# Moving one product of a pair's output projection behind the next scores, and the lower tiles' copies behind two exponentials, in a causal attention kernel in split fp32

## The chip, the cores and the metric

The kernel runs on one core of one Trainium2 chip. The metric is the device time of one execution in microseconds, and the number for the kernel before is the median of three executions, 1481.09 us (1480.62 to 1482.14).

## The reference, cut to what matters

The whole is one transformer block on x of 4 batches x 512 positions x 512 channels: an adaptive layer norm, causal attention with 32 heads of 128 channels (8 key and value heads, each shared by 4 heads) and rotary positions, a gated residual, a second norm, and a mixture over 64 expert biases with the 8 largest router weights. The change lies in the attention:

```python
q = (h @ Wq.T) ...                    # 32 heads of 128, then rotary
scores = einsum('bhqd,bhkd->bhqk', q, k) * scale       # causal
attn = softmax(scores)
out = einsum('bhqk,bhkd->bhqd', attn, v)
return out.reshape(..., 32 * 128) @ Wo.T               # "the projection"
```

All of it is wanted in fp32. The kernel gets this out of fp32r products by splitting each operand into a high and a low part and running three products (low times high, high times low, high times high) for one, which `passes` (line 94) lists.

## The kernel before, in words

**Steps.** Work is cut into 32 units (a key and value head and a batch), each with 4 heads. One head of one unit is a step, t = 0 to 127; h = t % 4, u = t // 4. The loop `for t in range(BY_PE)` is unrolled on each engine, and every engine has its own hand-written order in a function `step(t)`. In one step TensorE computes the scores of head t + 1, the queries of head t + 3 (`q_proj`, 12 products), in steps with h = 1 and 3 the keys and values of the next unit, and parts of what belongs to earlier heads. From step 92 (`FFN_FROM`) on the second half of the block (norm, router, experts), for tiles that are finished, is mixed in as well. The change leaves these later steps as they are.

**Pairs.** After the softmax two heads are handled together as a pair p (heads 2p and 2p + 1). The 512 queries are four tiles of 128: UPPER is tiles 2 and 3, LOWER is tiles 0 and 1. `values_pair(p, UPPER)` writes probabilities times values to the PSUM bank pv in step 2p + 2, `values_pair(p, LOWER)` does the same in step 2p + 3. ScalarE copies the bank to OT_hi (`pair_split_hi`, L1059) and VectorE writes the remainder OT_lo (`pair_split_lo`, L1433). UPPER and LOWER use the same two OT buffers, one after the other. `out_pair(p, UPPER)` (L718) then runs 12 products of 512 columns at the end of step 2p + 3, and `out_pair(p, LOWER)` another 12 in step 2p + 4, into the banks o0 to o3. ScalarE may overwrite OT with LOWER only once the UPPER products have read it: it waits on the semaphore `pe_upper` or `pe_op`, which the last product of tile 3 increments.

**TensorE, one even step t = 2p + 4 (before).** scores(t + 1) in tile order 3, 2, 1, 0 (L649, L645 and, last, L646); q_proj(t + 3) (L589); out_pair(p, LOWER); values_pair(p + 1, UPPER). The scores of tile 3 and the queries share the bank s3, so `q_proj` waits until VectorE has read tile 3's scores (`dve_s`, L1393). `out_pair(p, LOWER)` waits for OT_lo (`dve_o`). An odd step has scores, values_pair LOWER, q_proj, keys or values, out_pair UPPER.

**ScalarE, one even step.** `pair_split_hi` LOWER (L1059); `split_moved_hi(t - 1)` (L1049, two copies of 640 columns from PT_raw to PT_hi); `exponentials(t + 1, 0)` of tiles 3 and 2 (L1028), which wait for VectorE's minima; `exponentials(t + 1, 1)` of tiles 1 and 0; `normalise` (L1035) in two halves, each after VectorE's `invert_sums` (L1400).

**VectorE, one even step.** `mask_and_max(t + 1, 0)` reads the scores of tiles 3 and 2 (L1393); `pair_split_lo` LOWER (L1433); `mask_and_max(t + 1, 1)` of tiles 1 and 0; in h = 2 two sums into y (`add_out`, L1450); `invert_sums`; `q_rope(t + 3)` (L1355 to L1357), which waits for the queries; the transposes of the normalised probabilities in 32 x 32 blocks (L1417).

**The transposed probabilities.** They leave by DMA to DRAM (`store_blocks`, L2010) and come back reordered (`load_transposed`, L2036) as PT_raw. In an odd step t SP issues the eight loads of heads t - 1 and t, four each, as soon as `values_pair` LOWER has finished with the buffers (`pe_pv`). ScalarE splits head t - 1 at the end of the odd step and head t in the next even step (L1049); GpSimd makes the low parts (L1759).

The queues of the engines are in order: an instruction waits for its semaphore and what stands behind it waits too.

Of the kernel before, what the change touches and what calls it, by code (L numbers as in the profile page):

```python
# [12 lines left out]
P = 128  # L13
BATCH, SEQ, HID = 4, 512, 512
HEADS, KV, HD = 32, 8, 128
GROUP = HEADS // KV
# [119 lines left out]
def build(nc, A, out):  # L136
    ctx = ExitStack()
    with ctx:
# [373 lines left out]
        def tensor_program(pe):  # L512
# [159 lines left out]
            def values_pair(p, tiles):  # L672
# [24 lines left out]
                                       start=(kb == 0 and n == 0), stop=(kb == last_key and n == 2))  # L697
                mm.then_inc(pe_pv, 1)

            def out_pair(p, tiles, some=None):  # L700
                u = 2 * p // GROUP
                heads = [2 * p % GROUP, 2 * p % GROUP + 1]
                pe.wait_ge(dve_o, pair_done(p, tiles))
                for h in heads:
                    wait_weights(u, f"wo{h}")
                if p == 0:

                    if tiles == UPPER:
                        pe.wait_ge(dve_r, 6)
                    else:  # L710
                        pe.wait_ge(dve_vt, 2)
                for j in some or tiles:
                    if heads[0] == 0 and 0 < u < LAST_UNIT:
                        pe.wait_ge(dve_y, added(u - 1, j))
                    for h in heads:
                        o_at = (2 * (j - tiles[0]) + h % 2) * P
                        for n, (o, w) in enumerate(passes(OT_of(p, tiles), wo)):
                            mm = pe.matmul(bank[f"o{j}"][:], o[:, o_at:o_at + P], w[:, h, :],  # L718
                                           start=(u < LAST_UNIT and h == 0 and n == 0),
                                           stop=(u < LAST_UNIT - 1 and h == GROUP - 1 and n == 2))  # L720
                    if heads[1] == GROUP - 1:
                        mm.then_inc(pe_op, 1)
                    elif j == UPPER[-1]:
                        mm.then_inc(pe_upper, 1)

            def values_last(t, tiles):
# [77 lines left out]
            def step(t):  # L804
                u, h, n, before = t // GROUP, t % GROUP, ffn_tile(t), ffn_tile(t - 1)
                scores(t + 1, QUERY_ORDER, before, n)
                if h % 2 == 1 and t > 1:
                    values_pair(t // 2 - 1, LOWER)
                if 2 < t < ALL - 3:
                    q_proj(t + 3)  # L810
                if h == 1 and 0 < u < LAST_UNIT:
                    k_proj(u + 1)
                if h == 3 and 0 < u < LAST_UNIT:
                    v_proj(u + 1)

                if t == 0:
                    q_proj(4)
                    k_proj(1)
                if t == 1:
                    v_proj(1)  # L820
                    q_proj(5)
                if h % 2 == 1 and t > 1:
                    out_pair(t // 2 - 1, UPPER)
                if n is not None:
                    pe.wait_ge(dve_s, score_read(t + 1, 0))
                    ffn_mix(early(n - 4), "s1")
                    ffn_logits(early(n - 2), "s2")
                if h % 2 == 0 and t > 2:
                    out_pair(t // 2 - 2, LOWER)
                if n is not None:  # L830
                    tile_waits((mixed, n - 4), last=EARLY_TILES - 1)
                    ffn_transpose(early(n - 1), "s1")
                if h % 2 == 0 and t > 0:
                    values_pair(t // 2 - 1, UPPER if t < ALL - 2 else LOWER)
                if before is not None:
                    pe.wait_ge(dve_s, score_read(t + 1, 0))
                    ffn_weights_T(early(before - 3), "s1")
# [103 lines left out]
        def scalar_program(act):  # L941
# [181 lines left out]
            def step(t):  # L1123
                u, h, n, before = t // GROUP, t % GROUP, ffn_tile(t), ffn_tile(t - 1)
                if h % 2 == 1 and t > 1:
                    pair_split_hi(t // 2 - 1, UPPER)
                if h % 2 == 0 and 2 < t < ALL - 2:
                    pair_split_hi(t // 2 - 2, LOWER)
                if t == 1:
                    split_moved_hi(0)  # L1130
                if h % 2 == 1 and t + 2 < ALL:
                    q_split(t + 2)
                if t == 2:
                    k_split(1)
                if h % 2 == 0 and 0 < t < ALL - 2:
                    split_moved_hi(t - 1)
                if t == ALL - 2:
                    split_moved_hi(t - 2)
                    split_moved_hi(t - 1)
                if n is not None:  # L1140
                    ffn_exp(early(n - 3))
                if t == 0:
                    v_split_hi(0)
                exponentials(t + 1, 0)
                if h == 1 and t > 1:
                    v_split_hi(u)
                exponentials(t + 1, 1)
                if n is not None:
                    ffn_normal(early(n - 1))
                if t == ALL - 3:  # L1150
                    pair_split_hi(PAIRS - 2, LOWER)
                normalise(t + 1, 0)
                if t == 2:
                    q_split(4)
                if h == 2 and 0 < u < LAST_UNIT:
                    k_split(u + 1)
                normalise(t + 1, 1)
                if h % 2 == 1 and 1 < t < ALL - 3:
                    split_moved_hi(t - 1)
                if h % 2 == 1 and 1 < t < ALL - 3:  # L1160
                    q_split(t + 3)
                for g, i in pieces(t):
                    split_chunk(g, i)
                if n is not None:
                    ffn_modulate(early(n - 1), "s1")
                if t - FFN_FROM in EXPERT_STEPS:
                    split_experts(EXPERT_STEPS.index(t - FFN_FROM))
                if t == ALL - 4:
                    make_diagonal()
                if before is not None:  # L1170
                    ffn_weights_copy(early(before - 3), "s1")
# [97 lines left out]
        def vector_program(dve):  # L1269
# [291 lines left out]
            def step(t):  # L1561
                u, h, n, before = t // GROUP, t % GROUP, ffn_tile(t), ffn_tile(t - 1)
                if h % 2 == 1 and t > 1:
                    pair_split_lo(t // 2 - 1, UPPER)
                mask_and_max(t + 1, 0)
                if t == 1:
                    mask_and_max(2, 1)
                    k_rope(1)
                    invert_sums(2, 0)
                    invert_sums(2, 1)  # L1570
                    split_moved_lo(0)
                    transpose_blocks(2)
                    return
                if h % 2 == 0 and 2 < t < ALL - 2:
                    pair_split_lo(t // 2 - 2, LOWER)
                mask_and_max(t + 1, 1)
                if t == ALL - 2:
                    split_moved_lo(t - 1)
                if before is not None:
                    ffn_x1(early(before))  # L1580
                    ffn_stats(early(before))
                if h == 2 and 0 < u < LAST_UNIT:
                    add_out(u - 1, UPPER)
                if h == 3 and 0 < u < LAST_UNIT:
                    add_out(u - 1, LOWER)
                if t == 2:
                    q_rope(4)
                invert_sums(t + 1, 0)
                if h == 1:
                    v_split_lo(u)  # L1590
                if 2 < t < ALL - 3:
                    q_rope(t + 3)
                invert_sums(t + 1, 1)
                if t == 0:
                    v_split_lo(0)
                if t == ALL - 3:
                    pair_split_lo(PAIRS - 2, LOWER)
                if h % 2 == 1:
                    transpose_blocks(t + 1, QUERY_ORDER[:2])
                if h == 1 and u + 1 < UNITS:  # L1600
                    k_rope(u + 1)
                if h == 3 and u + 1 < UNITS:
                    transpose_values(u + 1)
                if n is not None:
                    finish(early(n - 4), "s1")
                    ffn_top(early(n - 3))
                    ffn_bias(early(n - 2), "s2")
                    keep(early(n - 3))
                if h % 2 == 1:
                    transpose_blocks(t + 1, QUERY_ORDER[2:])  # L1610
                elif moved(t + 1):
                    transpose_blocks(t + 1)
                if t in (0, 2):
                    q_rope(t + 3)
# [631 lines left out]
```

## Time and profile before

| | before |
|---|---|
| median of 3 runs | 1481.09 us |
| the profiled execution, its own time | 1481.78 us |
| span of its trace, first to last instruction | 1480.1 us |
| TensorE busy (matmuls) | 1451.2 us, 98% |
| VectorE busy | 1160.1 us, 78% |
| GpSimd busy | 1023.6 us, 69% |
| ScalarE busy | 1005.0 us, 68% |
| granted TensorE clock, mean | 0.996 |

1.7 us of the profiled execution's own time lie outside the span. Busy time is the union of the records of an engine; matmuls overlap in the records (each is drawn some 390 ns long while the next starts 230 ns later), so a busy TensorE can still lose time between the starts of two products. That is why the rows below are start times of single products.

### The profile page before, as it was taken

Reading aid. Unit: us, or ns where it says so; the run is one execution under the profiler, and the core shown is the slowest. Engines: PE = TensorE matmul, PEld = TensorE weight load, DVE = VectorE, ACT = ScalarE, POOL = GpSimd, SP = SyncE. Lnnn points to the kernel's source line nnn. Section 1 sums busy time; section 2 is a strip of 40 time slices with the busy share of each in tenths; the row PEclk is TensorE's granted clock in tenths of the full one; section 3 lists DMA queues with packets and bytes.
Section 4 is the critical chain, followed back from the end, with each engine's and each line's share of the span. In section 5 each row is a group of like instructions: output and inputs, shape, how many; then the busy total and the mean of one; then the engine's idle time right before and its main releaser. Section 6 shows DMA issues by size and latency. Waiting matters only on the chain.

```text
span 1480.1 us, 24295 instructions
## 1 busy us (share of the span) xinstructions
PE 1451.2 (98%) x7012; PEld 1211.3 (82%) x7012; DVE 1160.1 (78%) x3549; ACT 1005.0 (68%) x2381; POOL 1023.6 (69%) x802
## 2 busy tenths in 40 slices
PE   7997999999999999999999999999999999999997
PEld 4686888888888888888888888888888888888876
DVE  5867777777777777777777777777779988988866
ACT  2467776776767776777677766767677676776674
POOL 1656776776667776677678666767588888886662
PEclk9999999999999999999999999999999999999999
DMA  9647775776766676578667756669788899889881
GB/s 328 205 126 255 223 229 144 213 224 182 202 216 214 181 223 188 172 219 237 182 184 222 220 168 199 213 180 254 224 248 252 270 293 260 278 263 266 268 228 51
DMA packets 214820, 322.02 MB, mean 218 GB/s; under 512 B 42248, under 2 KB 132104, under 8 KB 214688
## 3 DMA queue, kind: packets, MB, share of 16 engines
q1 hardware_dynamic: 214352, 320.34, 72.3%
q8 instruction: 57, 0.93, 0.3%
q14 instruction: 75, 0.61, 0.1%
q10 hardware_dynamic: 336, 0.12, 0.0%
HBM read 179.43 MB, written 140.95 MB: 216 GB/s over the span
## 4 chain that ended last, share of the span: by engine, by line
PE 90%; DVE 5%; issue 2%; ACT 2%; POOL 1%; DMA 0%; SPq 0%; DVEq 0%; ACTq 0%; POOLq 0%
PE bank_s L589 22%; PE bank_o L718 22%; PE bank_pv L696 14%; PE bank_s L649 13%; PE bank_s L617 6%; PE bank_s L602 5%; PE bank_s L560 2%; PE bank_o L523 1%; PE bank_s L645 1%; PE bank_s L771 1%; DVE blocks L1417 1%; ACT probs L1028 1%; PE bank_pv L589 1%; DMA wup_in<-in_wup 0%; PE bank_s L646 0%
## 5 line engine op out<-in xcount | busy, mean ns | idle before, releaser
L1759 POOL TENSOR_TENSOR PT_lo<-PT_raw,PT_hi 128x640 fp32r<-128x640 f32 x246 | 382.1, 1574 | 27.0 <-ACT PT_hi L1049 27.0
L1035 ACT ACTIVATE probs<-probs,row_inv 128x512 f32<-128x512 f32 (+3 forms) x512 | 258.0, 553 | 195.2 <-DVE row_inv L1400 195.1
L1747 POOL TENSOR_TENSOR rot_c<-rot_c,rot_s 128x512 f32<-128x512 f32 x128 | 166.0, 1297 | 274.3 <-DVE rot_s L1357 274.3
L1028 ACT ACTIVATE probs<-probs,row_min 128x512 f32<-128x512 f32 (+3 forms) x512 | 281.8, 552 | 52.2 <-DVE row_min L1393 52.1
L1417 DVE STREAM_TRANSPOSE blocks<-probs 128x384 f32<-128x384 f32 x508 | 213.9, 447 | 18.7 <-ACT probs L1035 12.4
L649 PE MATMUL bank_s<-kT_both,qT_hi 128*128 128x512 f32 (+2 forms) x768 | 214.9, 341 | 1.2 <-POOL qT_lo L1752 0.6
L1393 DVE CUSTOM_DVE_ANT_0 probs<-bank_s,mask 128x512 f32<-128x512 f32 (+2 forms) x384 | 203.5, 552 | 0.4
L589 PE MATMUL bank_s<-hT_lo,wq_hi 128*128 128x512 f32 x488 | 196.5, 403 | 2.5 <-DVE row_min L1393 1.2
L1752 POOL TENSOR_TENSOR qT_lo<-rot_c,qT_hi 128x512 fp32r<-128x512 f32 x128 | 166.6, 1301 | 42.2 <-ACT qT_hi L1010 41.3
L718 PE MATMUL bank_o<-wo_lo,OT_hi 128*128 128x512 f32 x496 | 194.4, 392 | 0.0
L718 PE MATMUL bank_o<-wo_hi,OT_hi 128*128 128x512 f32 x496 | 193.3, 390 | 0.0
L718 PE MATMUL bank_o<-wo_hi,OT_lo 128*128 128x512 f32 x496 | 192.9, 389 | 0.0
L589 PE MATMUL bank_s<-hT_hi,wq_hi 128*128 128x512 f32 x488 | 191.3, 392 | 0.0
L589 PE MATMUL bank_s<-hT_hi,wq_lo 128*128 128x512 f32 x488 | 190.4, 390 | 0.0
L1049 ACT ACTIVATE PT_hi<-PT_raw 128x640 fp32r<-128x640 f32 x250 | 169.7, 728 | 12.9 <-DMA PT_raw<-blocks 12.4
L649 PEld LDWEIGHTS bank_s<-kT_both,qT_hi 128*128 128x128 f32 x768 | 142.6, 188 | 17.3 <-DVE kv_rot L1366 1.8
L1433 DVE TENSOR_TENSOR OT_lo<-bank_pv,OT_hi 128x512 fp32r<-128x512 f32 x124 | 85.4, 688 | 83.7 <-ACT OT_hi L1059 83.7
L696 PE MATMUL bank_pv<-PT_lo,v_hi 128*128 128x512 f32 x374 | 138.8, 371 | 9.6 <-issue 5.5
L1355 DVE TENSOR_TENSOR rot_c<-bank_s,cos_t 128x512 f32<-128x512 f32 x122 | 84.2, 690 | 80.8 <-PE bank_s L589 78.3
L696 PE MATMUL bank_pv<-PT_hi,v_hi 128*128 128x512 f32 x374 | 133.9, 358 | 0.0
L696 PE MATMUL bank_pv<-PT_hi,v_lo 128*128 128x512 f32 x374 | 133.8, 358 | 0.0
L649 PE MATMUL bank_s<-kT_both,qT_lo 128*128 128x512 f32 (+2 forms) x384 | 129.3, 337 | 0.0
(296 smaller groups left out, 3216.6 us busy)
## 6 DMA issues: line engine op xcount, KB each, us to landing
blocks<-blocks SPq DMA_DIRECT2D x127, 640.0 KB, 3.4
PT_raw<-blocks SPq DMA_DIRECT2D x500, 160.0 KB, 3.9
stage<-in_wq SPq DMA_DIRECT2D x32, 256.0 KB, 5.1
vblocks<-kv_raw SPq DMA_DIRECT2D x32, 256.0 KB, 5.4
kv_raw<-vblocks SPq DMA_DIRECT2D x128, 64.0 KB, 2.1
stage<-in_wo SPq DMA_DIRECT2D x32, 256.0 KB, 5.0
split_wq<-wq_hi SPq DMA_DIRECT2D x32, 256.0 KB, 5.4
split_wq<-wq_lo SPq DMA_DIRECT2D x32, 256.0 KB, 5.7
```

Source lines behind the costliest of these rows:

```text
L589: mm = pe.matmul(q_bank(t)[:], w[:, h, c, :], x[:, b * CH + c, :], start=(c == 0 and n == 0), stop=(c == CH - 1 and n == 2))
L649: mm = pe.matmul(score_bank[qt], q, k[:, 0:keys], start=(n == 0), stop=(n == 2))
L696: mm = pe.matmul(to[:, :, (first - tiles[0]) * SUB:], a[:, kb, :], ps, start=(kb == 0 and n == 0), stop=(kb == last_key and n == 2))
L718: mm = pe.matmul(bank[f"o{j}"][:], o[:, o_at:o_at + P], w[:, h, :], start=(u < LAST_UNIT and h == 0 and n == 0), stop=(u < LAST_UNIT - 1 a ...
L1028: ins = act.activation(row(t, qt), row(t, qt), ACT.Exp, bias=row_min[m][:, qt:qt + 1], scale=-1.0, accum_out=row_sum[m][:, qt:qt + 1])
L1035: ins = act.activation(row(t, qt), row(t, qt), ACT.Copy, scale=row_inv[t % 2][:, qt:qt + 1])
L1049: act.activation(parts_of(t)[0][:, at], raw_of(t)[:, at], ACT.Copy).then_inc(act_t, 1)
L1393: dve.tensor_tensor_reduce(row(t, qt), score_bank[qt], row(t, 0) if qt == 0 else mask[:, SEQ - (qt + 1) * P:], -SCALE, -LOWEST, ALU.add, A ...
L1417: ins = dve.transpose(blocks_v[:, qt:qt + 3 * whole_keys - 2:3], keys[:, 0:whole_keys])
L1747: pool.tensor_tensor(rot_c[:], rot_c[:], rot_s[:], ALU.add).then_inc(pool_a, 1)
L1752: pool.tensor_tensor(lo[:], rot_c[:], hi[:].bitcast(F32), ALU.subtract).then_inc(pool_q, 1)
L1759: pool.tensor_tensor(lo[:, at], raw_of(t)[:, at], hi[:, at].bitcast(F32), ALU.subtract).then_inc(pool_t, 1)
```

## The change

In the even steps 4 to 90, the product high times high of the second head on tile 3 of `out_pair(p, UPPER)` is no longer issued at the end of step 2p + 3 but in step 2p + 4, between the scores and the queries. The increment of `pe_upper` or `pe_op` goes with it. ScalarE's copy of the LOWER pair moves from the front of the even step to behind `exponentials(t + 1, 0)`; VectorE's remainder moves from between the two halves of `mask_and_max` to behind both. From step 92 on all stays as it was. No instruction is added or removed.

```diff
+            def upper_in_two(p):
+                return 2 * p + 4 < FFN_FROM
+
             def out_pair(p, tiles, some=None):
...
                     for h in heads:
-                        o_at = (2 * (j - tiles[0]) + h % 2) * P
-                        for n, (o, w) in enumerate(passes(OT_of(p, tiles), wo)):
-                            mm = pe.matmul(...)
-                    if heads[1] == GROUP - 1:
+                        put_off = j == UPPER[-1] and h == heads[1] and upper_in_two(p)
+                        out_head(p, tiles, j, h, range(2) if put_off else range(3))
+
+            def out_head(p, tiles, j, h, which):
+                u = 2 * p // GROUP
+                o_at = (2 * (j - tiles[0]) + h % 2) * P
+                for n, (o, w) in enumerate(passes(OT_of(p, tiles), wo)):
+                    if n in which:
+                        mm = pe.matmul(...)
+                if 2 in which:
+                    if h == GROUP - 1:
                         mm.then_inc(pe_op, 1)
-                    elif j == UPPER[-1]:
+                    elif h == 1 and j == UPPER[-1]:
                         mm.then_inc(pe_upper, 1)
...
# TensorE, step(t)
                 if h % 2 == 1 and t > 1:
                     values_pair(t // 2 - 1, LOWER)
+                if h % 2 == 0 and t > 2 and upper_in_two(t // 2 - 2):
+                    p = t // 2 - 2
+                    out_head(p, UPPER, UPPER[-1], 2 * p % GROUP + 1, range(2, 3))
                 if 2 < t < ALL - 3:
                     q_proj(t + 3)
# ScalarE, step(t)
-                if h % 2 == 0 and 2 < t < ALL - 2:
+                if h % 2 == 0 and FFN_FROM <= t < ALL - 2:
                     pair_split_hi(t // 2 - 2, LOWER)
...
                 exponentials(t + 1, 0)
                 if h == 1 and t > 1:
                     v_split_hi(u)
+                if h % 2 == 0 and 2 < t < FFN_FROM:
+                    pair_split_hi(t // 2 - 2, LOWER)
                 exponentials(t + 1, 1)
# VectorE, step(t)
-                if h % 2 == 0 and 2 < t < ALL - 2:
+                if h % 2 == 0 and FFN_FROM <= t < ALL - 2:
                     pair_split_lo(t // 2 - 2, LOWER)
                 mask_and_max(t + 1, 1)
+                if h % 2 == 0 and 2 < t < FFN_FROM:
+                    pair_split_lo(t // 2 - 2, LOWER)
```

## Rows read from the trace of the kernel before

**Rows 1.** The page's busy time of each engine: busy us (share of the span) xinstructions.

```profile
PE 1451.2 (98%) x7012; PEld 1211.3 (82%) x7012; DVE 1160.1 (78%) x3549; ACT 1005.0 (68%) x2381; POOL 1023.6 (69%) x802
```

**Rows 2.** Timeline of TensorE around step 50: start us, length, engine, line, operation, tiles.

```profile
613.43 0.39 PE L718 MATMUL bank_o<-wo_hi,OT_hi 128*128 128x512 f32 x1
613.65 0.39 PE L649 MATMUL bank_s<-kT_both,qT_hi 128*128 128x512 f32 x1
...
615.34 0.22 PE L646 MATMUL bank_s<-kT_both,qT_lo 128*128 128x128 f32 x1
615.52 0.47 PE L589 MATMUL bank_s<-hT_lo,wq_hi 128*128 128x512 f32 x1
615.83 0.40 PE L589 MATMUL bank_s<-hT_hi,wq_lo 128*128 128x512 f32 x1
...
618.34 0.39 PE L718 MATMUL bank_o<-wo_lo,OT_hi 128*128 128x512 f32 x1
```

**Rows 3.** The same view, odd step 51: scores, then a product that waits for nothing.

```profile
625.17 0.22 PE L646 MATMUL bank_s<-kT_both,qT_lo 128*128 128x128 f32 x1
625.23 0.45 PE L696 MATMUL bank_pv<-PT_lo,v_hi 128*128 128x512 f32 x1
625.52 0.39 PE L696 MATMUL bank_pv<-PT_hi,v_lo 128*128 128x512 f32 x1
```

**Rows 4.** The same view, even step 48, the shorter kind of wait.

```profile
594.49 0.22 PE L646 MATMUL bank_s<-kT_both,qT_lo 128*128 128x128 f32 x1
594.62 0.47 PE L589 MATMUL bank_s<-hT_lo,wq_hi 128*128 128x512 f32 x1
```

**Rows 5.** Timeline of ScalarE and VectorE, step 50 to the start of step 51.

```profile
613.91 0.60 ACT L1059 ACTIVATE OT_hi<-bank_pv 128x512 fp32r<-128x512 f32 x1 [0.59 <-PE bank_o L718]
614.41 1.35 ACT L1049 ACTIVATE PT_hi<-PT_raw 128x640 fp32r<-128x640 f32 x2
...
615.29 0.08 DVE L1393 DVE_READ_ACCUMULATOR2_ANT row_min<- 128x1 f32 x1
...
615.78 0.69 DVE L1433 TENSOR_TENSOR OT_lo<-bank_pv,OT_hi 128x512 fp32r<-128x512 f32 x1
...
617.14 1.28 DVE L1450 TENSOR_TENSOR y<-bank_o,y 128x512 f32<-128x512 f32 x2
...
623.69 0.60 ACT L1059 ACTIVATE OT_hi<-bank_pv 128x512 fp32r<-128x512 f32 x1 [0.34 <-PE bank_pv L696]
...
624.32 0.69 DVE L1433 TENSOR_TENSOR OT_lo<-bank_pv,OT_hi 128x512 fp32r<-128x512 f32 x1 [1.34 <-ACT OT_hi L1059]
```

**Rows 6.** Timeline of ScalarE in step 20, where the load of PT_raw is late.

```profile
301.58 1.37 ACT L1049 ACTIVATE PT_hi<-PT_raw 128x640 fp32r<-128x640 f32 x2 [0.65 <-DMA PT_raw<-blocks]
302.86 0.71 ACT L1028 ACTIVATE probs<-probs,row_min 128x512 f32<-128x512 f32 x1
...
303.56 0.60 ACT L1028 ACTIVATE probs<-probs,row_min 128x384 f32<-128x384 f32 x1
```

**Rows 7.** The same view: first and last of the ten even steps with such a wait.

```profile
176.02 1.37 ACT L1049 ACTIVATE PT_hi<-PT_raw 128x640 fp32r<-128x640 f32 x2 [0.33 <-DMA PT_raw<-blocks]
...
845.15 1.37 ACT L1049 ACTIVATE PT_hi<-PT_raw 128x640 fp32r<-128x640 f32 x2 [0.76 <-DMA PT_raw<-blocks]
```

**Rows 8.** ScalarE's waits from 155 to 1050 us: us in total, times, longest.

```profile
ACT PT_hi L1049 <- DMA PT_raw<-blocks: 6.6, 16, 0.8
```

**Rows 9.** The view of tile PT_raw around step 50, issues and landing.

```profile
L2036 SPq DMA_DIRECT2D PT_raw<-blocks x8: 303/432/1172, 605.7 to 609.6; - x8
...
DMA to landing us min/median/max: 2.5/3.6/4.4
```

**Rows 10.** DMA queues from 295 to 297 us (step 20): packets, MB, share.

```profile
q8 instruction: 1, 0.02, 4.2%
```

**Rows 11.** Timeline of TensorE in step 4.

```profile
133.02 0.22 PE L646 MATMUL bank_s<-kT_both,qT_lo 128*128 128x128 f32 x1
134.43 0.47 PE L589 MATMUL bank_s<-hT_lo,wq_hi 128*128 128x512 f32 x1 [1.18 <-DVE row_min L1393]
```

More of the change, by code:

```diff
@@ L715, in out_pair @@
                     for h in heads:
-                        o_at = (2 * (j - tiles[0]) + h % 2) * P
-                        for n, (o, w) in enumerate(passes(OT_of(p, tiles), wo)):
-                            mm = pe.matmul(bank[f"o{j}"][:], o[:, o_at:o_at + P], w[:, h, :],
-                                           start=(u < LAST_UNIT and h == 0 and n == 0),
-                                           stop=(u < LAST_UNIT - 1 and h == GROUP - 1 and n == 2))
-                    if heads[1] == GROUP - 1:
+                        put_off = j == UPPER[-1] and h == heads[1] and upper_in_two(p)
[5 more added lines that the diff above has]
+                    if n in which:
+                        mm = pe.matmul(bank[f"o{j}"][:], o[:, o_at:o_at + P], w[:, h, :],
+                                       start=(u < LAST_UNIT and h == 0 and n == 0),
+                                       stop=(u < LAST_UNIT - 1 and h == GROUP - 1 and n == 2))
+                if 2 in which:
+                    if h == GROUP - 1:
                         mm.then_inc(pe_op, 1)
-                    elif j == UPPER[-1]:
+                    elif h == 1 and j == UPPER[-1]:
                         mm.then_inc(pe_upper, 1)
```

## The prediction

> **What bounds the kernel now.** I read the page's busy times first: TensorE is busy for 98% of the span, no other engine for more than 78% [rows 1]. So a gain can only come from the spacing of TensorE's products, and a loss from any wait put in front of them. About 0.2%, 3 us, is what a measurement of this kernel can tell from no change.
>
> Then I went through TensorE's timeline step by step. Every time below is against T, the start of the last score product (L646) of an even step; in step 50, T = 615.34. There the first query product starts at T + 0.18 and the second 0.31 later [rows 2]. In an odd step the product behind the scores waits for nothing: it starts 0.06 after L646 and the next 0.29 later [rows 3] (0.284 as the mean over the odd steps; from here on three digits are means over the start times of all steps of a kind, of which one row stands). The even step's wait is for VectorE: its reading of tile 3 ends at 615.29 + 0.08 = T + 0.03 [rows 5], and TensorE starts 0.15 us after that. Of the 44 even steps that the change touches (4 to 90), 29 look like step 50, 13 have the shorter wait of step 48, 0.13 to 0.14 us [rows 4], and two (4 and 46) are irregular.
>
> **What is gained.** With the moved product in front, the order is L646, 0.06, moved product, 0.284, first query, 0.23, second query. The 0.23 that it took at the end of the odd step (613.43 to 613.65 [rows 2]) is gone there. Before, from L646 to the third query: 0.181 + 0.314 + 0.230, and 0.227 in the odd step, 0.952. After: 0.060 + 0.284 + 0.230 + 0.230 = 0.804. Gain 0.148. In the 13 shorter steps 0.096. The wait itself is hidden: it lets go at about T + 0.15 and the query now wants to start at T + 0.34. Sum: 29 x 0.148 + 13 x 0.096 = 5.5 us. Steps 4 and 46 give nothing: there VectorE itself is late, and the first query starts when VectorE lets it, in step 4 at T + 1.41 [rows 11]. Bounds: 5.5 us, and 0 if VectorE's read of tile 3 slips by as much as TensorE comes earlier; the nearest row is step 50, where that read begins behind a wait for TensorE, so I take 5.5.
>
> **The copies that move.** This is the other half, and I cost it by the chain that `out_pair` LOWER waits for. Today ScalarE copies LOWER at T - 1.43 (613.91), VectorE's remainder is done at 615.78 + 0.69 = T + 1.13 [rows 5], and the LOWER products start at 618.34 = T + 3.00 [rows 2]. There are 1.9 us of slack. After the change the copy stands behind three things on ScalarE: two PT copies, 1.27 us from the start of the first to the exponential (301.58 to 302.86), then the exponentials of tile 3, 0.71 to the start of the next (302.86 to 303.56), and tile 2, 0.60 [rows 6]. Then: OT_hi 0.60, hand-over 0.03 (623.69 + 0.60 to 624.32), OT_lo 0.69 [rows 5], and 0.15 to TensorE (the hand-over above). From the start of an exponential of tile 3 to the first LOWER product: 0.71 + 0.60 + 0.60 + 0.03 + 0.69 + 0.15 = 2.78 us. TensorE gets there at T + 0.06 + 0.28 + 12 x 0.229 = T + 3.09. So the exponential must start by T + 0.31.
>
> *When the loads are on time it does.* It then waits only for the minima, until about T + 0.07. The PT copies do not hold it: around step 50 the last load is issued at 609.6 and lands at most 4.4 us later [rows 9], at 614.0, T - 1.3. That load is released by the odd step's `values_pair`, and one product fewer now lies between that and T, so in the new frame it lands at T - 1.1, the PT copies end at T + 0.17, and 0.14 to 0.24 us are left.
>
> *When the loads are late it does not.* In ten of the 44 steps ScalarE, having finished OT_hi at T - 0.83, sits idle for d before it can start the PT copies: 0.33, 0.44, 0.20, 0.65, 0.66, 0.43, 0.50, 0.17, 0.21 and 0.76 us (steps 8, 16, 18, 20, 40, 42, 52, 60, 64, 72), 4.35 in all; step 20's row and the first and last of them are shown [rows 6, 7]. They are ten of the 16 waits of this kind [rows 8]; the other six are in odd steps or ahead of the even heads' copies and are not lengthened. Today these waits cost TensorE nothing, because the LOWER copy is ahead of them. Now it is behind: the exponential starts at T - 0.83 + d + 0.23 (the shorter frame) + 1.27 = T + 0.67 + d, and TensorE waits 0.36 + d. Sum: 10 x 0.36 + 4.35 = 7.9 us. In step 72 OT_hi ended 0.1 later than elsewhere, which makes 8.0.
>
> Loads that land inside the time that OT_hi covers today show no idle time. They cost from 0 up to 0.36 in each of 32 steps, 0 to 11 us. The nearest row is the load of step 50, which leaves a margin, so most cost nothing; for a handful of later ones (some 0.1 to 0.2 each) I take 0.7. A pipeline that restarts after a wait loses some 0.03 (0.314 against 0.284): 10 x 0.03 = 0.3. Step 4 is late in the loads as well as in VectorE: between 0 and 1.9 (today's slack); ScalarE's PT copies there end late enough that I take 1.4. Loss: 8.0 + 0.7 + 0.3 + 1.4 = 10.4 us.
>
> **What else moves.** VectorE's later work in an even step starts when OT_lo ends, T + 2.7 instead of T + 1.9. In h = 2 this delays the 1.28 us of `add_out`, the rotation and ScalarE's normalising by some 0.8; VectorE idles 1.34 us ahead of the next step's remainder [rows 5], so the transposes and the store still end in time, and I cost it at nothing; without that cover it would be 0.8 x 22 = 18 us. `add_out` now needs the moved product, which ends near T + 0.5, before VectorE can be there. `values_pair` UPPER needs the bank pv free at T + 5.7, 3 us after OT_lo. On GpSimd and SP nothing is moved.
>
> **Sum.** 10.4 - 5.5 = 4.9 us slower. Against the profiled execution, 1481.78 us, that is 1486.7; it ran 0.7 above the median, so 1486.0.
>
> **Rivals.**
>
> *A: the loads land early enough and the gain stays.* What lets a load be late? In step 20 one packet of 16 KB of the instruction queue runs in the middle of the loads [rows 10]. For A: late loads could be chance, fewer in the next program, or the margin 0.3 larger than I made it from single rows. If all ten were on time, 5.5 - 0.7 - 1.4 (step 4) = 3.4 to 5.5 us are gained: 1475.6 to 1477.7. Against A: ScalarE's wait would have to vanish from ten steps, and even d = 0 costs 0.36. Chance 0.17. The Trainium skill ("Runtime: NRT & Kernel Launch", Instruction fetch mechanics) says that crossing a 16 KiB block of instructions is one tail bump of the queue, "mostly hidden". By that rule the fetch would delay nothing and case A's time would hold; the trace shows the fetch among loads that are late, so I give it no more than A's chance.
>
> *B: gain and loss cancel.* If the chain is 0.2 to 0.3 shorter per step than my sum (a PT copy that starts sooner), the ten waits cost 5 to 6 us and steps at the margin nothing: from 3 faster to 3 slower, 1478.1 to 1484.1. Chance 0.22. The point from which it decides is a start of the exponential at T + 0.55 instead of T + 0.31.
>
> *C: every step waits.* The margin in steps with loads on time is only 0.15 to 0.25 us. If ScalarE or the hand-overs take 0.3 more than I read, 32 further steps wait 0.1 to 0.3 us: some 6 us more, 1490 to 1494. Chance 0.06.
>
> *D: the change does nothing*, because the query's wait is not the one for tile 3. The irregular step 4 names VectorE's minimum as what is waited for [rows 11], so this is inside B.
>
> The forecast has 0.55: 3 to 8.4 us slower, 1484.1 to 1489.5. Slower 0.55 + 0.06 = 0.61, same 0.22, faster 0.17. The range goes from 1477.5 to 1489.5: below it lies most of A (0.14), above it C (0.06).
>
> **What would show it.** Right: the product L718 between L646 and L589, the first query 0.34 after L646 without a wait; a new wait of L718 for DVE OT_lo (L1433), ten to fifteen times, up to 1.2 us, in the same steps in which ScalarE waits for PT_raw; some 9 us in all. Wrong: no such waits (A), waits in nearly all even steps (C), or the first query still late behind VectorE.

## The result and the profile after

The changed kernel takes 1484.45 us (median of 20 runs, 1480.36 to 1486.29) against 1481.05 us for the kernel before (20 runs, 1479.42 to 1482.75): a ratio of 1.0020, 95% interval 1.0013 to 1.0027. By the medians it is 3.4 us slower, at the near end of the 3 to 8.4 us of the forecast. The single run that was profiled took 1483.30 us (span 1481.6), below that median, so the trace shows less of the loss than the median has. The changed kernel also scatters more: 5.9 us from fastest to slowest instead of 3.3.

The page after. TensorE's busy time has fallen while the span has grown: the time without a product record went from 28.9 us (1480.1 - 1451.2) to 32.6 (1481.6 - 1449.0). The chain that ended last has changed as well; DMA has 5% of it, where it had 0% before:

```profile
PE 1449.0 (98%) x7012; PEld 1207.1 (81%) x7012; DVE 1155.9 (78%) x3549; ACT 1004.8 (68%) x2381; POOL 1023.5 (69%) x802
...
PE 82%; DVE 5%; DMA 5%; ACT 4%; SPq 2%; issue 2%; POOL 0%; DVEq 0%; ACTq 0%; POOLq 0%
PE bank_o L729 21%; PE bank_s L589 18%; PE bank_pv L696 14%; PE bank_s L649 12%; PE bank_s L617 4%; PE bank_s L602 4%; DMA PT_raw<-blocks 4%; SPq L2055 2%; PE bank_s L560 2%; ACT probs L1043 2%; PE bank_o L523 1%; PE bank_s L645 1%; PE bank_s L783 1%; ACT PT_hi L1064 1%; DVE OT_lo L1450 1%
```

The loads of PT_raw hold 4% of that chain now, with ScalarE's and VectorE's work behind them (L729 is the old L718, L1064 the old L1049, L1074 the old L1059, L1450 the old L1433). The next rows are TensorE's waits from 120 to 1060 us: us in total, times, longest.

```profile
PE bank_o L729 <- DVE OT_lo L1450: 3.4, 7, 0.8
```

The kernel before has no such wait. The view draws a wait only where it is longer than the overlap of the records, so I also took the start times of all products: in 12 of the 44 steps the first LOWER product comes later than 0.23 after the last query product, by 5.7 us in all, the longest 1.0. ScalarE's waits from 155 to 1050 us show what stands in front; against [rows 8] the wait for the loads has gone from 6.6 to 33.0 us. Most of it is time in which ScalarE used to copy LOWER, and costs nothing:

```profile
ACT PT_hi L1064 <- DMA PT_raw<-blocks: 33.0, 46, 1.3
```

**A step with its load on time**, step 50 again: timelines of TensorE, ScalarE and VectorE. These answer to [rows 2, 5].

```profile
616.67 0.22 PE L646 MATMUL bank_s<-kT_both,qT_lo 128*128 128x128 f32 x1
616.73 0.45 PE L729 MATMUL bank_o<-wo_hi,OT_hi 128*128 128x512 f32 x1
617.02 0.39 PE L589 MATMUL bank_s<-hT_lo,wq_hi 128*128 128x512 f32 x1
...
619.77 0.39 PE L729 MATMUL bank_o<-wo_lo,OT_hi 128*128 128x512 f32 x1
```

```profile
615.67 1.37 ACT L1064 ACTIVATE PT_hi<-PT_raw 128x640 fp32r<-128x640 f32 x2 [0.79 <-DMA PT_raw<-blocks]
616.95 0.71 ACT L1043 ACTIVATE probs<-probs,row_min 128x512 f32<-128x512 f32 x1
...
618.25 0.58 ACT L1074 ACTIVATE OT_hi<-bank_pv 128x512 fp32r<-128x512 f32 x1
...
618.86 0.69 DVE L1450 TENSOR_TENSOR OT_lo<-bank_pv,OT_hi 128x512 fp32r<-128x512 f32 x1 [0.85 <-ACT OT_hi L1074]
```

With T = 616.67: moved product at T + 0.06, first query at T + 0.35 without a wait, LOWER at T + 3.10. The PT copies start at T - 1.00, the exponential at T + 0.28, and OT_lo is done at T + 2.88. That is 0.22 before TensorE's arrival; less the hand-over of 0.06 (below) 0.16 are left, within the 0.14 to 0.24 that the prediction gave. In the other steps of this trace whose LOWER products don't wait, 0 to 0.34 are left.

**A step with a late load**, step 64: TensorE, then ScalarE and VectorE, then the chain that ended last in the same stretch.

```profile
762.92 0.22 PE L646 MATMUL bank_s<-kT_both,qT_lo 128*128 128x128 f32 x1
762.98 0.45 PE L729 MATMUL bank_o<-wo_hi,OT_hi 128*128 128x512 f32 x1
763.27 0.39 PE L589 MATMUL bank_s<-hT_lo,wq_hi 128*128 128x512 f32 x1
...
765.79 0.39 PE L589 MATMUL bank_s<-hT_hi,wq_hi 128*128 128x512 f32 x1
766.80 0.50 PE L729 MATMUL bank_o<-wo_lo,OT_hi 128*128 128x512 f32 x1 [0.62 <-DVE OT_lo L1450]
767.14 0.40 PE L729 MATMUL bank_o<-wo_hi,OT_lo 128*128 128x512 f32 x1
```

```profile
762.87 1.37 ACT L1064 ACTIVATE PT_hi<-PT_raw 128x640 fp32r<-128x640 f32 x2 [1.16 <-DMA PT_raw<-blocks]
764.14 0.70 ACT L1043 ACTIVATE probs<-probs,row_min 128x512 f32<-128x512 f32 x1
...
765.45 0.57 ACT L1074 ACTIVATE OT_hi<-bank_pv 128x512 fp32r<-128x512 f32 x1
...
766.05 0.69 DVE L1450 TENSOR_TENSOR OT_lo<-bank_pv,OT_hi 128x512 fp32r<-128x512 f32 x1 [1.85 <-ACT OT_hi L1074]
```

```profile
756.70 6.14 DMA PT_raw<-blocks
...
762.87 0.64 ACT PT_hi L1064
...
764.24 1.30 ACT probs L1043 x4
765.54 0.49 ACT OT_hi L1074
...
766.05 0.70 DVE OT_lo L1450
...
766.80 3.01 PE bank_o L729 x12
```

The load takes 6.14 us to land (4.4 at most in [rows 9]), ScalarE starts the PT copies at T - 0.05 instead of T - 1.00, and the LOWER products start 1.01 after the last query product instead of 0.23: a wait of 0.78. One packet of the instruction queue runs here too: by its record it starts at 756.56, 0.14 before the load is issued, and takes 1.29 us (DMA queues, 755 to 757.5 us):

```profile
q8 instruction: 1, 0.02, 3.2%
```

### The profile page after: what moved, and what is told of

It is laid out like the page before. It is cut to its first block, busy times and chain, and to the rows that moved or that the text cites. A ratio compares the mean times of both kernels' runs of the same rounds, so it can differ in the third digit from the quotient of the medians.

```text
span 1481.6 us, 24295 instructions
## 1 busy us (share of the span) xinstructions
PE 1449.0 (98%) x7012; PEld 1207.1 (81%) x7012; DVE 1155.9 (78%) x3549; ACT 1004.8 (68%) x2381; POOL 1023.5 (69%) x802
## 4 chain that ended last, share of the span: by engine, by line
PE 82%; DVE 5%; DMA 5%; ACT 4%; SPq 2%; issue 2%; POOL 0%; DVEq 0%; ACTq 0%; POOLq 0%
PE bank_o L729 21%; PE bank_s L589 18%; PE bank_pv L696 14%; PE bank_s L649 12%; PE bank_s L617 4%; PE bank_s L602 4%; DMA PT_raw<-blocks 4%; SPq L2055 2%; PE bank_s L560 2%; ACT probs L1043 2%; PE bank_o L523 1%; PE bank_s L645 1%; PE bank_s L783 1%; ACT PT_hi L1064 1%; DVE OT_lo L1450 1%
## 5 line engine op out<-in xcount | busy, mean ns | idle before, releaser
L729 PE MATMUL bank_o<-wo_lo,OT_hi 128*128 128x512 f32 x496 | 196.3, 396 | 5.7 <-DVE OT_lo L1450 3.4
L1064 ACT ACTIVATE PT_hi<-PT_raw 128x640 fp32r<-128x640 f32 x250 | 170.1, 729 | 39.2 <-DMA PT_raw<-blocks 38.5
L729 PE MATMUL bank_o<-wo_hi,OT_hi 128*128 128x512 f32 x496 | 196.3, 396 | 0.0
L589 PE MATMUL bank_s<-hT_lo,wq_hi 128*128 128x512 f32 x488 | 193.4, 396 | 1.9 <-DVE row_min L1410 0.9
L729 PE MATMUL bank_o<-wo_hi,OT_lo 128*128 128x512 f32 x496 | 193.1, 389 | 0.0
L1450 DVE TENSOR_TENSOR OT_lo<-bank_pv,OT_hi 128x512 fp32r<-128x512 f32 x124 | 85.6, 690 | 128.7 <-ACT OT_hi L1074 128.7
```

The source lines that it names most:

```text
L589: mm = pe.matmul(q_bank(t)[:], w[:, h, c, :], x[:, b * CH + c, :], start=(c == 0 and n == 0), stop=(c == CH - 1 and n == 2))
L1064: act.activation(parts_of(t)[0][:, at], raw_of(t)[:, at], ACT.Copy).then_inc(act_t, 1)
```

## The experiments

The change once more, the copies alone, the product alone and the other product put off were timed together, with the kernel before at 1481.51 us; the remaining four together on another chip, with it at 1482.29 us. Differences are between medians of the same session.

**The change once more.**

> The changed kernel once more, to see whether the waits of the LOWER products come back in the same steps. Theory (the LOWER copy stands behind a late load of PT_raw): 10 to 14 waits of out_pair for OT_lo, most of them again in steps 8, 20, 40, 42, 60, 64 and 84, their sum 5 to 8 us, and a time 2 to 5 us above the kernel before. Rival (the waits are chance of one execution): fewer than half of those steps wait again.

1486.02 us against 1481.51, ratio 1.0027 (1.0019 to 1.0036). Its trace has waits in 16 steps, 6.6 us in all; 11 of the first trace's 12 steps (4, 6, 8, 16, 20, 28, 40, 42, 60, 64, 84, and not 66) are among them. So the waits are tied to places in the program, but each one's size changes by some tenths: 1.0 us in step 8 of the first trace and 0.2 in the second. That would widen the scatter, but it is not shown to be all of it: the kernel with the product alone, where no LOWER product waits, scatters by 4.7 us over 11 runs. By the medians the change is 4.5 us slower here, near the forecast's 4.9.

**Only the copies moved.**

```diff
             def upper_in_two(p):
-                return 2 * p + 4 < FFN_FROM
+                return False
```

> Only the LOWER copies move, the product stays at the end of the odd step. Theory: the loss stays and the gain is gone; the queries wait again for tile 3 (first query 0.18 after the last score product), the LOWER products still wait after late loads, a little less each since the load is 0.23 earlier against the scores: 4 to 7 us above the kernel before, 1485 to 1488. Rival 1 (the product's new place costs the time, the copies are harmless): within 1 us of the kernel before. Rival 2 (the copies cost only because the product shortens the frame): 1 to 2 us above.

1487.54 us, ratio 1.0033 (1.0021 to 1.0046): 6.0 us slower than before. TensorE's waits from 120 to 1060 us:

```profile
PE bank_o L729 <- DVE OT_lo L1450: 4.3, 10, 0.7
```

By start times 11 steps wait, 6.2 us in all (the profiled run, 1489.38, is the slowest of the six). The kernel is slower without the product too, and its ratio can't be told from the 1.0027 with it. Both rivals fall: the copies are not harmless by themselves, and the product is not what costs. The gain is missing here, so the copies' own loss is 6.0 us, against 9.8 (4.5 + 5.3, below) beside the moved product; the late steps' shorter frame would make such a difference, but the intervals are too wide to show it.

**Only the product moved.**

```diff
# ScalarE and VectorE, step(t): both copies back where they were
-                if h % 2 == 0 and FFN_FROM <= t < ALL - 2:
+                if h % 2 == 0 and 2 < t < ALL - 2:
                     pair_split_hi(t // 2 - 2, LOWER)
...
-                if h % 2 == 0 and 2 < t < FFN_FROM:
-                    pair_split_hi(t // 2 - 2, LOWER)
```

> Only the product moves; ScalarE's LOWER copy is again ahead of the PT copies and so waits for the moved product until about 0.45 after the last score product, and holds back the PT copies and all exponentials of the step by some 1.9 us. Theory: no product of out_pair waits for OT_lo; the gain of 3 to 5 us shows unless the late exponentials reach TensorE through the stores and loads: 1477 to 1479. Rival (the product's place itself costs): 1481 or more, with the first query late. Second rival (late exponentials matter): above 1483, with waits of values_pair for PT_lo or of scores.

1481.70 us, ratio 0.9996 (0.9987 to 1.0005): no change, and outside the expected 1477 to 1479. The time is that of the first rival, but its sign is not there: the first query starts 0.35 after L646 in all steps but 4 and 46. No LOWER product waits. The second rival's time (above 1483) did not come, but a wait of the scores, which it named, did. The trace shows a new short stop in the steps with h = 2, here between steps 50 and 51, on GpSimd and on TensorE:

```profile
622.22 1.29 POOL L1783 TENSOR_TENSOR kT_both<-kv_raw,kT_both 128x512 fp32r<-128x512 f32 x1 [0.74 <-ACT kT_both L1031]
```

```profile
623.30 0.28 PE L696 MATMUL bank_pv<-PT_hi,v_hi 128*128 128x256 f32 x1
623.61 0.47 PE L649 MATMUL bank_s<-kT_both,qT_hi 128*128 128x512 f32 x1
623.92 0.39 PE L649 MATMUL bank_s<-kT_both,qT_lo 128*128 128x512 f32 x1
```

The same on GpSimd and the first score product in the kernel before:

```profile
621.69 1.31 POOL L1768 TENSOR_TENSOR kT_both<-kv_raw,kT_both 128x512 fp32r<-128x512 f32 x1 [0.74 <-ACT kT_both L1016]
```

```profile
623.49 0.39 PE L649 MATMUL bank_s<-kT_both,qT_hi 128*128 128x512 f32 x1
```

The scores of the next unit need the low part of its keys. Before, it is done at 621.69 + 1.31 = 623.00, 0.49 ahead of them; now at 622.22 + 1.29 = 623.51, and they start 0.31 after the product before them instead of 0.12, the next one 0.31 later instead of 0.23. ScalarE's LOWER copy waits for the moved product and starts at 615.81 instead of 613.91, the PT copies behind it are late, GpSimd's PT_lo starts at 617.11 instead of 616.59, and the keys queue up behind that.

**The product moved in the steps with h = 0 alone.**

```diff
             def upper_in_two(p):
-                return 2 * p + 4 < FFN_FROM
+                return 2 * p + 4 < FFN_FROM and p % 2 == 0
```

(on top of the kernel with the product alone moved)

> As the kernel with the product alone moved, but only in the even steps with h = 0 (22 of 44); in those with h = 2 it stays in the odd step. Theory (what product_only gives back is the wait of the next unit's first scores for the low part of the keys on GpSimd, which the late PT copies push back in steps with h = 2): the half without keys keeps its gain, 22 x 0.12 = 2.6 us, 1478 to 1479.5. Rival (the give-back is spread over all steps): within 1 us of the kernel before.

1478.97 us, ratio 0.9980 (0.9971 to 0.9989), 3.3 us faster than before. Half the steps give more than all 44 do. What comes back is lost from h = 2 on, as the trace said: by the starts of the scores, the product alone in all 44 steps is 0.25 us slower per unit in steps h = 2 and 3 than the kernel with the other product put off (below), and no slower in h = 0 and 1.

**ScalarE's chain 0.60 shorter.**

```diff
-                exponentials(t + 1, 0)
...
                 if h % 2 == 0 and 2 < t < FFN_FROM:
+                    exponentials(t + 1, 0, (3,))
                     pair_split_hi(t // 2 - 2, LOWER)
+                    exponentials(t + 1, 0, (2,))
```

> As the changed kernel, but ScalarE's LOWER copy goes behind the exponential of tile 3 alone, so 0.60 us earlier. Theory (the waits are the part of load lateness plus chain that exceeds TensorE's arrival): every wait is 0.60 shorter; of the 12 to 16 waits three to five are left, 1 to 2 us in all, and the gain shows: 1477 to 1479. Rival (the waits have another cause than the length of ScalarE's chain, such as VectorE's order): the time stays at 1484 to 1487.

1479.19 us, ratio 0.9978 (0.9969 to 0.9987), 0.2 us above what was expected. TensorE's waits, 120 to 1060 us:

```profile
PE bank_o L729 <- DVE OT_lo L1454: 1.0, 3, 0.7
```

By start times six steps wait, 2.0 us in all, three of them under 0.3. The loads are as late as before (ScalarE waits 34.0 us for them in this trace). So the length of the chain decides what a late load costs.

**ScalarE's chain 0.50 longer.**

```diff
                 if h % 2 == 0 and 2 < t < FFN_FROM:
+                    exponentials(t + 1, 1, (1,))
                     pair_split_hi(t // 2 - 2, LOWER)
-                exponentials(t + 1, 1)
+                    exponentials(t + 1, 1, (0,))
```

> As the changed kernel, but the LOWER copy goes behind the exponential of tile 1 too, 0.50 us later. Theory: the waits that there are grow by 0.5 each (14 x 0.5 = 7 us) and the margin of the steps with loads on time is used up, so that some 30 more steps wait 0.1 to 0.3 us and pay a restart of 0.15 each: 10 to 18 us above the changed kernel, 1495 to 1503. Rival (only late loads matter, the margin is wider): 7 us above, 1492.

1503.01 us, ratio 1.0144 (1.0130 to 1.0158), 20.7 us slower than before, at the end of what was expected.

```profile
PE bank_o L729 <- DVE OT_lo L1454: 13.8, 23, 1.3
```

By start times all 44 steps wait, 21.7 us in all, the shortest 0.15. So the margin in steps with loads on time was at most 0.35 us, and rival C of the prediction, waits in every step, lay one short operation away.

**The other product put off.** In this version the high times high product stays in the odd step and the one that reads OT_lo (low times high) is put off instead. ScalarE's OT_hi is free when the odd step ends, and both LOWER copies go back to their old places. Only VectorE, writing OT_lo, waits for the moved product (`upper_done(p)` in the cut below counts what the pairs before p have added to `pe_upper`).

```diff
             def out_head(p, tiles, j, h, which, low_last=False):
...
+                products = passes(OT_of(p, tiles), wo)
+                if low_last:
+                    products = [products[0], products[2], products[1]]
...
+                        if low_last and n == 1:
+                            mm.then_inc(pe_upper, 1)
...
# ScalarE, pair_split_hi
+                if tiles == LOWER and 2 * p + 4 < FFN_FROM:
+                    act.wait_ge(pe_upper, upper_done(p) + 1)
...
# VectorE, pair_split_lo
+                if tiles == LOWER and 2 * p + 4 < FFN_FROM:
+                    if p % 2 == 0:
+                        dve.wait_ge(pe_upper, upper_done(p) + 2)
+                    else:
+                        dve.wait_ge(pe_op, QT * (p // 2) + 2)
```

> The product put off is the one with the low part of OT (low times high), the high times high one stays in the odd step, and both LOWER copies are back at their old places. ScalarE overwrites OT_hi once the high products have read it, only VectorE's OT_lo waits for the moved product, until about 0.5 after the last score product, when it would start anyway (0.44). Theory: the gain of 3 to 5 us without the loss, 1476 to 1478, no wait of out_pair for OT_lo. Rival (the product's place itself costs): 1481 or more.

1475.79 us, ratio 0.9959 (0.9946 to 0.9971): 5.7 us faster than before and 10.2 faster than the change on the same chip. TensorE and VectorE in step 50 (L740 is the projection, L1468 OT_lo):

```profile
612.22 0.22 PE L654 MATMUL bank_s<-kT_both,qT_lo 128*128 128x128 f32 x1
612.27 0.46 PE L740 MATMUL bank_o<-wo_hi,OT_lo 128*128 128x512 f32 x1
612.57 0.40 PE L597 MATMUL bank_s<-hT_lo,wq_hi 128*128 128x512 f32 x1
```

```profile
612.71 0.08 DVE L1423 DVE_READ_ACCUMULATOR2_ANT row_min<- 128x1 f32 x1
612.84 0.69 DVE L1468 TENSOR_TENSOR OT_lo<-bank_pv,OT_hi 128x512 fp32r<-128x512 f32 x1
```

The moved product fills TensorE's gap. OT_lo starts 0.13 after the minimum is read out; before, both start at 615.78. So the new wait costs VectorE about 0.1 us. No LOWER product waits. From step 3 to step 90 TensorE comes out 5.4 us ahead of the trace before, of which 0.3 is an irregular stop in step 46 that this run did not have, while one in step 84 cost it 0.2.

**The same, in the later steps too.** The three bounds of 92 became 124.

> low_last with the product put off in the 16 even steps from 92 to 122 as well, where the first query starts 0.11 to 0.49 after the last score product. If the wait for tile 3 is hidden there too: 16 x 0.12 to 0.25 = 2 to 4 us less than low_last, 1472 to 1474. Rival (VectorE, busier in these steps, is late for other reasons and sets the pace): the same as low_last, 1475 to 1477.

1476.06 us, ratio 0.9958 (0.9946 to 0.9971), not to be told from the version above. In the trace the product is in its new place in the late steps (first query 0.35 after the last score product), but TensorE reaches the end of step 118 no earlier, counted from step 92: 6.6 us ahead of the kernel before at both. At the start of step 118 it is 7.3 ahead, 0.6 more than at step 92 where 2 to 4 us were expected, and in step 118 it loses 0.7 again, most of it in a stop inside the scores. The rival's time came out. Its reason, VectorE, isn't shown: the query's wait is hidden in all 16 steps. What sets the pace there I did not test.

## Why the prediction was right, point by point

**The gain.** 5.5 us were forecast (29 steps of 0.148, 13 of 0.096, nothing in 4 and 46). The version with the other product put off fills the same place, has the gain without the loss and shows 5.7 us by medians and some 5.3 by its trace. The step that hid the wait was right as well: the first query starts at T + 0.35 (forecast 0.34).

**The loss.** 10.4 us were forecast. In the trace of the change the net is +2.2 us from step 3 to step 91, so the loss is 2.2 + 5.3 = 7.5; in the second trace the net is +3.3 and the loss 8.6, and by the medians of the two sessions 3.4 + 5.3 = 8.7 and 4.5 + 5.3 = 9.8. The mechanism is the one named: late load, PT copies, two exponentials, OT_hi, OT_lo, first LOWER product, each seen in the chain of step 64, and moving the copy by one exponential either way moved the time by -7.6 or +16.2 us against the changed kernel (each taken as its difference to the kernel before in its own session: -3.1 and +20.7 against +4.5).

**What was mis-sized.** Four terms, which partly cancel:

| | forecast | first trace | second trace |
|---|---|---|---|
| the ten late steps | 8.0 | 3.7 | 3.9 |
| other steps | 0.7 | 1.3 | 2.0 |
| step 4 | 1.4 | 0.7 | 0.7 |
| beside the waits | 0.3 | 1.8 | 2.0 |
| loss, us | 10.4 | 7.5 | 8.6 |

The waits are from start times; the fourth row is the loss less the waits. The ten steps are too high for two reasons. The hand-over from VectorE to TensorE was taken as 0.15 us from the query's wait; behind OT_lo it is 0.06 (766.05 + 0.69 to 766.80), and the whole chain from the exponential to LOWER is 2.66 in step 64 (764.14 to 766.80) instead of 2.78. So a wait begins 0.12 later than I put it, 1.2 us over ten steps. And which loads are late is not fixed: steps 18, 52 and 72 were late in the trace before and did not wait in the first trace after, while 4, 6, 28, 66 and 84 did. A wait costs more than its length: I allowed 0.03 for a restart, but in step 64 the second product comes 0.34 after the first instead of 0.23 and the step as a whole loses 0.14 more than the wait.

That the time fell inside the range is in part luck. Of the signs that the prediction named, the number of waits came true (12 and 16, forecast ten to fifteen), but they are smaller: the longest 1.0 us (forecast 1.2), in all 5.7 and 6.6 us (some 9).

**The rivals.** A (loads early enough) is refuted by both runs of the change and by the copies alone. The Trainium skill ("Runtime: NRT & Kernel Launch", Instruction fetch mechanics) calls the cost of crossing a 16 KiB block of instructions mostly hidden. In step 20 before [rows 10] and in step 64 after one packet of the instruction queue runs beside the late load, so if the packet is the cause, its cost was not hidden from the load. In the three traces (before, after, after again) the loads of 15 even steps between 4 and 90 take over 5.7 us to land, and 14 of these steps have such a packet. The exception is step 78 of the second trace, and on-time steps such as 50 hold packets too. No run took the fetch away, so the cause of the late loads stays open. B (gain and loss cancel) was very near. Its waits of 5 to 6 us are what the first trace shows, and the first median, 3.4 us slower, is only 0.4 beyond B's 3; the second, 4.5, is clearer. What kept the time out of B was mostly the time lost beside the waits, which B did not have. C stayed out by margins of at most 0.35 us, 0.16 in step 50. D is out: the query's wait was for tile 3.

**What else moves** was costed at nothing, rightly for the change itself: nothing on TensorE waits but LOWER. But the keys' chain on GpSimd, which I did not look at, has so little slack (0.49 us before step 51) that the kernel with the product alone lost its whole gain there.

## What to carry to other kernels

When work is moved to fill a gap, cost the copies that have to move with it by the whole chain up to the engine that bounds the kernel, and start that chain at its least reliable member: a wait for a DMA that costs nothing today, because the critical copy stands in front of it, costs its full lateness once the copy stands behind. Before moving the copies, look at which operand the put-off product reads: here the product that reads the part written last, by the other engine, let every copy stay where it was. Where the margin is 0 to 0.35 us in a step that repeats 44 times, one operation more or less in the queue was worth 8 to 16 us.

## What was not expected of the hardware

The hand-over from VectorE to TensorE is not one number: 0.15 us from the end of the minimum to the first query product before, 0.06 from OT_lo's end to the LOWER product after, in every step that waits; why they differ was not tested. A stop of TensorE of 0.15 to 1.0 us costs 0.13 to 0.18 us beside its own length, in the eleven waiting steps of the first trace other than step 4. And the loads of PT_raw, which are late in about the same steps in each trace, are late by amounts that differ by tenths of a microsecond to nearly one from run to run. The kernel before scattered by 3.3 us over 20 runs (4.2 over 22 in the next session), the changed kernel by 5.9; whether the loads are the cause of the difference is not shown.
